# Scaled rows of batches 1 to 3 made on GpSimd, behind the subtraction of their step, instead of on ScalarE

## The chip, the cores and the metric

One core of a Trainium2 chip runs the kernel. The metric is the device time of one execution in microseconds (us), the median of several runs. The engines are TensorE (PE; its weight loads are PEld), VectorE (DVE), ScalarE (ACT), GpSimd (POOL) and SyncE (SP). Each works through its own list of instructions in order; they meet at semaphores.

## What is computed

Four batches of 256 tokens, 256 wide, go through two residual layers:

```
# layer 1: a sparse learned adjacency mixed with the normalised rows
sim  = (ctx Wq^T)(ctx Wk^T)^T * scale            # 256 x 256 per batch
A    = sigmoid(sim) where sim >= 76th largest of its row, else 0
x1   = x + (1-gamma) * layernorm(x) + gamma * (A + A^T) / 2
# layer 2: eight experts of 256 -> 256 -> 256, the best two of each token
xn   = layernorm(x1)
comb = weights of the two best gates of xn @ gate_w, zero for the rest, times alpha
out  = x1 + sum_e comb[e] * (gelu(xn @ fc1[e] + b1[e]) @ fc2[e] + b2[e])
```

`x + (1-gamma) * layernorm(x)` is, for each row, a factor times x plus a constant. These are the "scaled rows" of the title: `x_sb[b,t] = x_sb[b,t] * mul1 + add1`, with one `mul1` and one `add1` for each token.

## The kernel before

Tokens lie on the 128 partitions, so that a batch is 2 tiles of 128x256. All eight experts are computed for every token. Products of expert layers run on TensorE in a split form: each factor has a rounded part (`_hi`) and a remainder (`_lo`), and three products (hi·hi, lo·hi, hi·lo) are summed, which makes 12 matmuls of 256 columns for an `up` (L438, to `p_h`) and 12 for a `down` (L462, to `p_y`).

The expert part is one loop over 32 steps s = 8 b + e (batch b, expert e), written out by hand on each engine. TensorE does `up(s)` and, two steps later (LAG = 2), `down(s)`: the slot of step s holds `up(s)`, then `down(s - 2)`. ScalarE does `gelu(s)` (L576, to `h_act`) and `hidden_hi(s)` (L586, to `h_hi`). GpSimd does `hidden_lo(s)` (L708, the subtraction `h_lo = h_act - h_hi`). VectorE adds the weighted result of `down(s - 2)` to `acc` (`add_expert`, L1071).

The preparation of the next batch is woven into these steps. For batch b + 1, in the steps of batch b:

- e = 0 to 3, VectorE: search of the 76th largest value (counts, MAX8, MATCH_REPLACE8), at e = 2 also `ln1_affine` (L801: `mul1` and `add1`, semaphore `ln1_mul`), at e = 3 `choose` (L914) and `mask` (L958: `half = (sim >= threshold) * half`).
- e = 2, ScalarE: `sigmoid(b+1)` (L549, into `half`), then `base(b+1)` (L592), the scaled rows: two ACTIVATE of 128x256, in place in `x_sb`, released by `ln1_mul`.
- e = 3, GpSimd: `add_masked(b+1)` (L702: `x_sb += half`), when `masked` and `base_ready` are there.
- e = 5: TensorE turns `half` (L377) into `p_a`, VectorE adds it (`residual`, L973, to `x1`) and takes the moments; GpSimd computes `rstd` (L664); at e = 6 VectorE normalises (`normalise`, L987, to `xn`); at e = 7 TensorE transposes `xn` behind `up` (L386) and ScalarE and VectorE split it for the next batch (`xt_hi`, `xt_lo`).

Batch 0 is prepared ahead of the loop. Its scaled rows are made on GpSimd already, by a function of the same name (L682), with TENSOR_SCALAR; its `ln1_affine` is on GpSimd too (L690).

In the first batch the weights are still being split. For experts 2 to 7 ScalarE writes `-w_hi` into `w_lo` (`weight_neg`, L562), and GpSimd issues a DMA that adds `w` to it in memory (`weight_rest`, L673); for experts 4 to 7 it stands behind `hidden_lo` in steps 0 to 3. `up(e)` waits for its landing (L445). In step 4 ScalarE rounds the second biases (`b2_hi`, L649), and in step 5 VectorE combines them with two inputs in SBUF (`b2_parts_of`, L1059) ahead of `residual(1)`. Three more waits matter: `down(s)` waits until `add_expert(s - 2)` is done (L469), `gelu(s)` waits for `hidden_lo(s - 2)` (L580), and `up(s)` for `gelu(s - 2)` (L447).

Of the kernel before, what the change touches and what calls it, by code (L numbers as in the profile page):

```python
# [15 lines left out]
ACT = mybir.ActivationFunctionType  # L16
# [43 lines left out]
def xattn_moe_program(nc, x, attn, small, w, b2, out):  # L60
# [8 lines left out]
    TILES = N // P  # L69
# [13 lines left out]
    with ExitStack() as ctx:  # L83
        def sb(name, shape, dt=F32):
            return ctx.enter_context(nc.sbuf_tensor(name, shape, dt))
# [4 lines left out]
        def sem(name):  # L90
            return ctx.enter_context(nc.semaphore(name))
# [4 lines left out]
        x_sb = sb("x_sb", [P, BATCHES, TILES, HID])  # L96
# [52 lines left out]
        mul1 = sb("mul1", [P, BATCHES, TILES])  # L149
        add1 = sb("add1", [P, BATCHES, TILES])  # L150
# [93 lines left out]
        ln1_mul = sem("ln1_mul")  # L244
        base_ready = sem("base_ready")
# [268 lines left out]
        def _(act):  # L514
# [54 lines left out]
            def xt_hi_of(b):  # L569
                if b >= 2:  # L570
                    act.wait_ge(h_ready, (b - 1) * EXPERTS)
                for k in range(CH):
                    act.wait_ge(xn_t, b * CH + k + 1)
                    nc.scalar.activation(xt_hi[:, b % 2, k], XT_BANKS[k][:, 0:N], ACT.Copy).then_inc(xt_hi_ready, 1)
# [14 lines left out]
                    act.wait_ge(y_ready, s - LAG)  # L589
                nc.scalar.activation(h_hi[:, s % (LAG + 1)], h_act[:, s % 2], ACT.Copy).then_inc(h_hi_ready, 1)  # L590

            def base(b):  # L592

                act.wait_ge(ln1_mul, b + 1)
                for t in range(TILES):
                    last = nc.scalar.activation(x_sb[:, b, t], x_sb[:, b, t], ACT.Identity,
                                                scale=mul1[:, b, t:t + 1], bias=add1[:, b, t:t + 1])
                last.then_inc(base_ready, 1)

            def comb_hi_of(b):  # L600
                act.wait_ge(comb_tr, b + 1)
                nc.scalar.activation(comb_hi[:], COMB_T, ACT.Copy).then_inc(comb_hi_ready, 1)
# [26 lines left out]
            for s in range(STEPS):  # L629
                b, e = divmod(s, EXPERTS)  # L630
                more = b + 1 < BATCHES
                if e == 7 and more:
                    xt_hi_of(b + 1)
                gelu(s)
                if e == 0:
                    act.wait_ge(logits_t_ready, b + 1)
                    nc.scalar.activation(logits_t[:], LOGITS_T, ACT.Copy).then_inc(logits_t_copied, 1)
                hidden_hi(s)
                if e == (2 if b else 1):

                    act.wait_ge(gap_ready, b + 1)
                    nc.scalar.activation(gap_th[:], gap[:], ACT.Tanh, scale=0.5).then_inc(gap_th_ready, 1)
                if s < 2:
                    weight_neg(4 + s)
                if s in (1, 3):
                    weight_neg(6 + s // 2)
                if s == 4:
                    act.wait_ge(b2_in, 16)
                    nc.scalar.activation(b2_hi[:], b2_sb[:], ACT.Copy).then_inc(b2_hi_ready, 1)  # L649
                if e == 2 and more:  # L650
                    sigmoid(b + 1)
                    base(b + 1)
                if e == 5:
                    comb_hi_of(b)
                if e == 4 and b + 2 < BATCHES:
                    spread_of(b + 2)
                if e == 6 and b + 2 < BATCHES:
                    signs_of(b + 2)
                if e == 7 and b + 2 < BATCHES:
                    signs_again_of(b + 2)  # L660

        @block.gpsimd
        def _(pool):
            def rstd(veps, rs, b, veps_ready, ready):  # L664

                pool.wait_ge(veps_ready, (b + 1) * TILES)
                nc.gpsimd.tensor_tensor(rs[:, b, :], veps[:, b, :], neg_half[:], ALU.pow).then_inc(ready, 1)  # L667

            def weight_hi(e):
                pool.wait_ge(w_in[e], 16)  # L670
                nc.gpsimd.tensor_copy(w_hi[:, e], w_sb[:, e]).then_inc(w_hi_early, 1)  # L671

            def weight_rest(e):  # L673
                pool.wait_ge(w_neg_ready, e - 1)
                nc.gpsimd.dma_start(w_lo[:, e], w[:, e].bitcast(F32R), accum_op=ALU.add).then_inc(w_rest_in[e], 16)  # L675

            def weight_lo(e, j):
                pool.wait_ge(w_hi_early, e + 1)
                nc.gpsimd.tensor_tensor(w_lo[:, e, j], w_sb[:, e, j], w_hi[:, e, j],  # L679
                                        ALU.subtract).then_inc(w_lo_ready[e][j], 1)  # L680

            def base(b):  # L682

                pool.wait_ge(ln1_mul, b + 1)
                for t in range(TILES):
                    last = nc.gpsimd.tensor_scalar(x_sb[:, b, t], x_sb[:, b, t], mul1[:, b, t:t + 1],
                                                   add1[:, b, t:t + 1], ALU.mult, ALU.add)
                last.then_inc(base_ready, 1)

            def ln1_affine(b):  # L690

                pool.wait_ge(gam_ready, 1)
                pool.wait_ge(ln1_agg, (b + 1) * TILES)
                pool.wait_ge(ln1_rstd, b + 1)
                for t in range(TILES):
                    nc.gpsimd.tensor_scalar(mul1[:, b, t:t + 1], rstd1[:, b, t:t + 1], gam[:, 2:3], ones[:], ALU.mult,
                                            ALU.add)
                    last = nc.gpsimd.tensor_scalar(add1[:, b, t:t + 1], mv1[:, b, t, 0:1], gam[:, 3:4],
                                                   rstd1[:, b, t:t + 1], ALU.mult, ALU.mult)
                last.then_inc(ln1_mul, 1)  # L700

            def add_masked(b):  # L702

                pool.wait_ge(masked, (b + 1) * TILES)
                pool.wait_ge(base_ready, b + 1)
                nc.gpsimd.tensor_tensor(x_sb[:, b], x_sb[:, b], half[:, b], ALU.add).then_inc(base_sum, 1)

            def hidden_lo(s):  # L708
                pool.wait_ge(h_hi_ready, s + 1)
                if s > LAG:  # L710
                    pool.wait_ge(y_ready, s - LAG)
                nc.gpsimd.tensor_tensor(h_lo[:, s % (LAG + 1)], h_act[:, s % 2], h_hi[:, s % (LAG + 1)],  # L712
                                        ALU.subtract).then_inc(h_lo_ready, 1)

            nc.gpsimd.memset(neg_half[:], -0.5).then_inc(const_set, 1)
            nc.gpsimd.memset(ones[:], 1.0).then_inc(const_set, 1)
            pool.wait_ge(const_set, 2)
            nc.gpsimd.memset(comb_parts[:].bitcast(F32), 0.0).then_inc(rows_cleared, 1)
            nc.gpsimd.memset(b2_parts[:].bitcast(F32), 0.0).then_inc(rows_cleared, 1)
            weight_hi(0)  # L720
            rstd(veps1, rstd1, 0, ln1_veps, ln1_rstd)
            weight_lo(0, 0)
            weight_hi(1)
            weight_hi(2)
            ln1_affine(0)
            base(0)
            pool.wait_ge(chosen_ready, TILES)
            weight_lo(1, 0)
            weight_rest(2)
            pool.wait_ge(gate_hi_ready, 1)  # L730
            nc.gpsimd.tensor_tensor(gate_parts[:, :, 1], gate_sb, gate_parts[:, :, 0], ALU.subtract).then_inc(
                gate_lo_ready, 1)
            weight_lo(0, 1)
            rstd(veps2, rstd2, 0, ln2_veps, ln2_rstd)
            pool.wait_ge(xn_ready, TILES)
            weight_rest(3)
            weight_lo(1, 1)
            weight_hi(6)
            rstd(veps1, rstd1, 1, ln1_veps, ln1_rstd)
            for s in range(STEPS):  # L740
                b, e = divmod(s, EXPERTS)
                more = b + 1 < BATCHES
                if s < STEPS - 1:
                    hidden_lo(s)
                if s < 4:
                    weight_rest(4 + s)
                if s == 1:
                    weight_hi(7)
                if more and b and e == 0:
                    rstd(veps1, rstd1, b + 1, ln1_veps, ln1_rstd)  # L750
                if more and e == 3:
                    add_masked(b + 1)
                if more and e == 5:
                    rstd(veps2, rstd2, b + 1, ln2_veps, ln2_rstd)
                    pool.wait_ge(xn_ready, (b + 2) * TILES)
# [483 lines left out]
```

## Time and profile before

| | |
|---|---|
| median of 3 runs | 129.93 us (129.92 to 130.35) |
| the profiled execution | 129.84 us |
| its span, first to last instruction | 128.0 us |
| TensorE busy | 119.6 us |
| VectorE busy | 95.3 us |
| ScalarE busy | 85.8 us |
| GpSimd busy | 68.4 us |
| granted TensorE clock, mean | 0.996 of full speed |

The busy times are sums over the span and tell which engine has room, not which one sets the end. For that there is the chain of work that ended last, followed back from the last instruction. 1.84 us of the profiled execution lie outside of the span. Records of neighbouring instructions on one engine overlap by some tenths of a us, since each is a pipeline; the distance between two starts is what an instruction costs its engine.

### The profile page before, as it was taken

How to read it: one execution, taken by the hardware profiler on the slowest of the kernel's cores; microseconds unless marked ns; L12 is line 12 of the kernel's file. 1: busy time of each engine (PE TensorE's matmuls, PEld its weight loads, DVE VectorE, ACT ScalarE, POOL GpSimd, SP SyncE). 2: the span in 40 equal slices, each digit the busy share in tenths (PEclk: the TensorE clock that was granted, in tenths of full speed). 3: DMA queues.
4: the chain of work that ended last, by engine and by line, in shares of the span. 5: the costliest groups of instructions: out<-in, count | busy, mean ns of one | idle time of the engine just before them, and what ended most of it. 6: DMA issues, size and time to landing. Idle time of an engine off the chain costs nothing.

```text
span 128.0 us, 2762 instructions
## 1 busy us (share of the span) xinstructions
PE 119.6 (93%) x901; PEld 109.6 (86%) x901; DVE 95.3 (74%) x399; ACT 85.8 (67%) x210; POOL 68.4 (53%) x72
## 2 busy tenths in 40 slices
PE   6796897899899999999999999999999999999990
PEld 3353565799889999999999999999999999999990
DVE  0068899989976999999979899998766228623481
ACT  4279898899999778464987774857546544555510
POOL 2019987799949644652396256506952544444400
PEclk9999999999999999999999999999999999999998
DMA  1999987675998400010000000200000002000002
GB/s 61 200 365 419 405 321 109 83 145 70 196 177 132 88 0 3 0 60 28 5 0 0 5 0 3 82 3 5 0 0 0 5 0 82 0 5 0 3 0 82
DMA packets 3381, 10.05 MB, mean 78 GB/s; under 512 B 397, under 2 KB 869, under 8 KB 3365
## 3 DMA queue, kind: packets, MB, share of 16 engines
q0 software_dynamic: 864, 3.15, 15.1%
q1 hardware_dynamic: 2500, 6.71, 14.6%
q8 instruction: 7, 0.11, 0.4%
q14 instruction: 10, 0.07, 0.2%
HBM read 8.81 MB, written 1.05 MB: 77 GB/s over the span
## 4 chain that ended last, share of the span: by engine, by line
PE 69%; DVE 8%; DMA 7%; ACT 6%; POOL 4%; issue 2%; DVEq 0%; POOLq 0%
PE p_y L480 31%; PE p_h L458 30%; DMA w_lo<-w 5%; DMA attn_sb<-attn 2%; POOL w_lo L679 2%; DVE acc L1084 2%; ACT act_waste L546 2%; ACT h_act L582 1%; DVE top L907 1%; PE p_g L406 1%; PE p_a L382 1%; POOL h_lo L712 1%; PE p_s L342 1%; ACT h_hi L590 1%; PE p_a L335 1%
## 5 line engine op out<-in xcount | busy, mean ns | idle before, releaser
L712 POOL TENSOR_TENSOR h_lo<-h_act,h_hi 128x512 fp32r<-128x512 f32 x31 | 40.3, 1303 | 41.0 <-ACT h_hi L590 37.2
L582 ACT ACTIVATE h_act<-p_h,small_sb 128x256 f32<-128x256 f32 x64 | 26.7, 468 | 21.9 <-PE p_h L458 21.8
L458 PE MATMUL p_h<-xt_hi,w_hi 128*128 128x256 f32 x128 | 33.3, 282 | 0.8 <-DMA w_lo<-w 0.7
L1084 DVE SCALAR_TENSOR_TENSOR acc<-p_y,comb,acc 128x256 f32<-128x256 f32 x55 | 24.0, 476 | 12.6 <-PE p_y L480 11.9
L458 PE MATMUL p_h<-xt_hi,w_lo 128*128 128x256 f32 x128 | 32.9, 279 | 0.0
L480 PE MATMUL p_y<-w_hi,h_hi 128*128 128x256 f32 x126 | 26.0, 288 | 0.0
L458 PE MATMUL p_h<-xt_lo,w_hi 128*128 128x256 f32 x128 | 25.5, 280 | 0.0
L458 PEld LDWEIGHTS p_h<-xt_hi,w_hi 128*128 128x128 f32 x128 | 24.1, 188 | 1.5 <-DMA w_lo<-w 1.1
L480 PE MATMUL p_y<-w_hi,h_lo 128*128 128x256 f32 x126 | 25.3, 282 | 0.0
L480 PE MATMUL p_y<-w_lo,h_hi 128*128 128x256 f32 x126 | 25.2, 281 | 0.0
L458 PEld LDWEIGHTS p_h<-xt_hi,w_lo 128*128 128x128 f32 x128 | 24.0, 188 | 0.0
L590 ACT ACTIVATE h_hi<-h_act 128x512 fp32r<-128x512 f32 x32 | 20.2, 630 | 0.9
L458 PEld LDWEIGHTS p_h<-xt_lo,w_hi 128*128 128x128 f32 x128 | 19.6, 187 | 0.1
L480 PEld LDWEIGHTS p_y<-w_hi,h_hi 128*128 128x128 f32 x126 | 19.3, 188 | 0.2
L480 PEld LDWEIGHTS p_y<-w_lo,h_hi 128*128 128x128 f32 x126 | 19.4, 188 | 0.0
L480 PEld LDWEIGHTS p_y<-w_hi,h_lo 128*128 128x128 f32 x126 | 19.3, 188 | 0.0
L671 POOL CAST w_hi<-w_sb 128x1024 fp32r<-128x1024 f32 x5 | 5.7, 1151 | 7.6 <-DMA w_sb<-w 7.6
L667 POOL TENSOR_TENSOR rstd<-veps,neg_half 128x2 f32<-128x2 f32 x8 | 6.4, 799 | 1.1 <-DVE veps L782 1.1
L358 PE MATMUL p_y<-warm 128*128 128x256 bf16 x27 | 5.5, 378 | 1.2 <-DVE warm L1096 1.2
L567 ACT ACTIVATE w_lo<-w_hi 128x1024 fp32r<-128x1024 f32 x6 | 6.2, 1047 | 0.5 <-POOL w_hi L671 0.5
L907 DVE MAX8 top<-left 128x8 f32<-128x256 f32 x16 | 5.9, 408 | 0.4 <-DVE left L912 0.4
L675 POOL DMA_DIRECT2D w_lo<-w x6 | 5.5, 913 | 1.1 <-DVE xn L992 1.1
(143 smaller groups left out, 185.2 us busy)
## 6 DMA issues: line engine op xcount, KB each, us to landing
w_sb<-w SPq DMA_DIRECT2D x8, 512.0 KB, 8.5
w_lo<-w POOLq DMA_DIRECT2D x6, 512.0 KB, 5.6
x_sb<-x SPq DMA_DIRECT2D x1, 768.0 KB, 8.7
out<-acc SPq DMA_DIRECT2D x3, 256.0 KB, 2.5
x_sb<-x SPq DMA_DIRECT2D x1, 256.0 KB, 4.3
out<-acc SPq DMA_DIRECT2D x2, 128.0 KB, 2.0
attn_sb<-attn SPq DMA_DIRECT2D x1, 192.0 KB, 4.8
small_sb<-small SPq DMA_DIRECT2D x1, 97.5 KB, 4.4
```

The lines of the kernel that those rows point to most:

```text
L358: nc.tensor.matmul(p_y[1][:, 0:N], warm[:, 0:P], warm[:], start=True, stop=True)
L458: last = nc.tensor.matmul(dst, w_[:, e, 0, k, c * P:(c + 1) * P], v[:, b % 2, k, :], start=n == 0, stop=n == len(trio) - 1)
L480: last = nc.tensor.matmul(dst, v[:, s % (LAG + 1), k, t * P:(t + 1) * P], w_[:, e, 1, k, :], start=n == 0, stop=n == len(trio) - 1)
L567: nc.scalar.activation(w_lo[:, e], w_hi[:, e], ACT.Copy, scale=-1.0).then_inc(w_neg_ready, 1)
L582: last = nc.scalar.activation(h_act[:, s % 2, c], tiled(p_h[s % 2])[:, c, :], ACT.Gelu, bias=b1_sb[:, e, c:c + 1])
L590: nc.scalar.activation(h_hi[:, s % (LAG + 1)], h_act[:, s % 2], ACT.Copy).then_inc(h_hi_ready, 1)
L667: nc.gpsimd.tensor_tensor(rs[:, b, :], veps[:, b, :], neg_half[:], ALU.pow).then_inc(ready, 1)
L671: nc.gpsimd.tensor_copy(w_hi[:, e], w_sb[:, e]).then_inc(w_hi_early, 1)
L675: nc.gpsimd.dma_start(w_lo[:, e], w[:, e].bitcast(F32R), accum_op=ALU.add).then_inc(w_rest_in[e], 16)
L712: nc.gpsimd.tensor_tensor(h_lo[:, s % (LAG + 1)], h_act[:, s % 2], h_hi[:, s % (LAG + 1)], ALU.subtract).then_inc(h_lo_ready, 1)
L907: step_of_tile(nc.vector.max(top[:, t, 8 * r:8 * r + 8], left[:, t]))
L1084: last = nc.vector.scalar_tensor_tensor(acc[:, b % 2, t], tiled(y_bank(s, t))[:, t, :], comb[:, b, t, 0, e:e + 1], so_far, ALU.mult, ALU.add)
```

## The change

On ScalarE the function `base` and its call at e = 2 go. On GpSimd `base(b + 1)`, the function that has served batch 0, is called at e = 2 for batches 1 to 3, behind `hidden_lo(s)` and, in the first batch, behind the DMA issue of `weight_rest(6)`. It waits for `ln1_mul` from VectorE and increments `base_ready`, for which `add_masked` waits on GpSimd itself.

```diff
@@ scalar engine
-            def base(b):
-
-                act.wait_ge(ln1_mul, b + 1)
-                for t in range(TILES):
-                    last = nc.scalar.activation(x_sb[:, b, t], x_sb[:, b, t], ACT.Identity,
-                                                scale=mul1[:, b, t:t + 1], bias=add1[:, b, t:t + 1])
-                last.then_inc(base_ready, 1)
-
@@ scalar engine, loop over s
                 if e == 2 and more:
                     sigmoid(b + 1)
-                    base(b + 1)
@@ gpsimd, loop over s
                 if s == 1:
                     weight_hi(7)
+                if more and e == 2:
+                    base(b + 1)
                 if more and b and e == 0:
                     rstd(veps1, rstd1, b + 1, ln1_veps, ln1_rstd)
```

## Rows read from the trace of the kernel before

**Rows 1.** Chain that ended last, in order of time: start us, us, what.

```profile
31.09 6.54 DMA w_lo<-w
...
37.68 1.69 PE p_h L458 x12
...
120.66 1.44 PE p_y L480 x12
```

**Rows 2.** Groups by line and shape, ScalarE and GpSimd: count | busy us, mean ns.

```profile
L596 ACT ACTIVATE x_sb<-x_sb,add,mul 128x256 f32<-128x256 f32 x6 | 3.3, 592 | 3.2 <-DVE add L807 3.2
...
L686 POOL TENSOR_SCALAR x_sb<-x_sb,mul,add 128x256 f32<-128x256 f32 x2 | 1.1, 552 | 0.1
```

**Rows 3.** Timeline of ScalarE, steps 2 to 5: start us, us, line, what.

```profile
34.41 1.08 ACT L596 ACTIVATE x_sb<-x_sb,add,mul 128x256 f32<-128x256 f32 x2
35.40 0.81 ACT L582 ACTIVATE h_act<-p_h,small_sb 128x256 f32<-128x256 f32 x2
...
40.41 0.81 ACT L582 ACTIVATE h_act<-p_h,small_sb 128x256 f32<-128x256 f32 x2
```

**Rows 4.** Timeline of GpSimd, steps 2 to 5; idle before an instruction in brackets.

```profile
34.45 0.86 POOL L675 DMA_DIRECT2D w_lo<-w  x1
36.97 1.27 POOL L712 TENSOR_TENSOR h_lo<-h_act,h_hi 128x512 fp32r<-128x512 f32 x1 [1.66 <-ACT h_hi L590]
38.20 0.87 POOL L675 DMA_DIRECT2D w_lo<-w  x1
38.81 1.57 POOL L706 TENSOR_TENSOR x_sb<-x_sb,half 128x512 f32<-128x512 f32 x1
40.06 1.57 POOL L712 TENSOR_TENSOR h_lo<-h_act,h_hi 128x512 fp32r<-128x512 f32 x1
41.95 1.29 POOL L712 TENSOR_TENSOR h_lo<-h_act,h_hi 128x512 fp32r<-128x512 f32 x1 [0.33 <-ACT h_hi L590]
```

**Rows 5.** Landing of the DMA issued at 38.20, and TensorE's step 7.

```profile
w_lo<-w POOLq DMA_DIRECT2D x1, 512.0 KB, 5.5
...
44.13 0.28 PE L458 MATMUL p_h<-xt_hi,w_hi 128*128 128x256 f32 x1
```

**Rows 6.** Timeline of VectorE, steps 2 to 6.

```profile
32.98 0.25 DVE L807 TENSOR_SCALAR add<-mv,gam,rstd 128x1 f32<-128x1 f32 x1
...
34.93 0.88 DVE L962 SCALAR_TENSOR_TENSOR half<-sim,threshold,half 128x256 f32<-128x256 f32 x2
...
39.55 2.37 DVE L1063 SCALAR_TENSOR_TENSOR b_parts<-b_hi,small_sb,b_sb 24x256 fp32r<-24x256 f32 x1 [1.25 <-ACT b_hi L649]
...
44.77 0.73 DVE L992 TENSOR_SCALAR xn<-x,mv,rstd 128x256 f32<-128x256 f32 x2
```

**Rows 7.** Timeline of TensorE: the third of four transposes of `xn`, second tile.

```profile
45.77 0.27 PE L394 MATMUL p_x<-small_sb,xn 128*128 128x128 f32 x1
```

**Rows 8.** Timelines of GpSimd and VectorE ahead of the loop; last row: durations min/median/max.

```profile
11.99 2.01 POOL L671 CAST w_hi<-w_sb 128x1024 fp32r<-128x1024 f32 x2
13.29 0.73 DVE L877 SCALAR_TENSOR_TENSOR missed<-count,few 128x2 f32<-128x2 f32 x1
17.09 1.27 POOL L679 TENSOR_TENSOR w_lo<-w_sb,w_hi 128x512 fp32r<-128x512 f32 x1 [0.61 <-DVE chosen L918]
L970 DVE TENSOR_TENSOR x_sb<-x_sb,half x2: 429/663/897, 17.7 to 18.6; 128x256 f32<-128x256 f32 x2
```

**Rows 9.** Timelines of ScalarE, GpSimd, VectorE and TensorE, preparation of batch 2.

```profile
60.18 1.10 ACT L596 ACTIVATE x_sb<-x_sb,add,mul 128x256 f32<-128x256 f32 x2 [1.60 <-DVE add L807]
62.74 1.30 POOL L712 TENSOR_TENSOR h_lo<-h_act,h_hi 128x512 fp32r<-128x512 f32 x1 [4.40 <-ACT h_hi L590]
61.84 0.88 DVE L962 SCALAR_TENSOR_TENSOR half<-sim,threshold,half 128x256 f32<-128x256 f32 x2
62.64 1.85 DVE L1084 SCALAR_TENSOR_TENSOR acc<-p_y,comb,acc 128x256 f32<-128x256 f32 x4
64.89 0.48 PE L480 MATMUL p_y<-w_hi,h_hi 128*128 128x256 f32 x2
```

## The prediction, written before the change was run

> **What bounds the kernel now.** I read the chain that ended last first. From 37.68 to 122.1 us it is TensorE's `up` and `down` products and its small transposes, one behind the other with no other engine between; its entrance is the DMA of one weight remainder, issued by GpSimd at 31.09 and landed at 37.6, for which `up(5)` waited [rows 1]. So two things can make this kernel faster: something that lets that DMA land earlier, or fewer matmuls. And one thing makes it slower: any operand that comes to TensorE late after 37.68. Then I read the other engines' timelines only for that question: at each meeting point with TensorE, how early was the operand.
>
> **What is removed.** Six ACTIVATEs of 592 ns go from ScalarE [rows 2]. In the first batch the pair starts at 34.41 and the `gelu` behind it at 35.40, so ScalarE's list moves up by 0.99 us, until `gelu(5)`, which started at 40.41 and will start at 39.42 [rows 3]; I take it that `up(5)`, begun at 37.68 and 1.69 long [rows 1], has just ended then. In batch 2 (and batch 3 alike) ScalarE also idled 1.60 us for `ln1_mul` ahead of the pair, with `gelu(11)` queued behind [rows 9]; both go. But TensorE waited for neither: it is on the chain without a gap there. Gain at the end: 0. The whole removal lies after the issue at 31.09, so the entrance DMA isn't moved either.
>
> **What is added.** Two TENSOR_SCALARs per batch on GpSimd, the very form that made batch 0's rows, at 552 ns [rows 2], 1.10 us a batch.
>
> *First batch.* `ln1_mul` is there at 33.23 [rows 6]: no wait. The DMA issue at 34.45 occupies the list for 0.61 us (38.20 to 38.81, the same issue), so the pair starts at 35.06 and is done at 36.16. GpSimd idled 1.66 us there, until 36.97 [rows 4]. `hidden_lo(3)` queued behind can start when `h_hi(3)` is there, 36.97 - 0.99 = 35.98, so it starts at about 36.16, 0.8 earlier than before. Behind it stands the DMA issue of the last weight: 36.16 + 1.23 = 37.39 instead of 38.20. Before, it landed after 5.5 us at 43.7 and `up(7)` needed it at 44.13 [rows 5]: 0.4 us of room, now 1.2. Then `add_masked(1)` at 38.0 and `hidden_lo(4)` at 39.25 by the same distances [rows 4].
>
> *Batches 2 and 3.* Here `base` does wait: `ln1_mul` comes where ScalarE started its pair, at 60.18, so GpSimd works on the pair until 61.28, with `hidden_lo(11)` queued behind. `h_hi(11)` is early now, so `hidden_lo(11)` runs 61.28 to 62.6, before it began at 62.74 [rows 9]. The wait replaces a longer one. Cost 0.
>
> **A cost that no single row of the moved operation shows.** VectorE instructions that read two SBUF tensors get stuck behind GpSimd work. A 429 ns addition took 897 ns when a GpSimd subtraction ran from 17.09 to 18.36, ending 0.3 us after it; a 128x2 operation took 0.73 us from 13.29 and ended at 14.02, where GpSimd's CASTs (one input) ended at 14.00 [rows 8]; and `b2_parts_of`, on only 24 partitions, took 2.37 us from 39.55 to 41.92, through two GpSimd instructions back to back, and ended in the 0.33 us gap ahead of the third [rows 4, 6]. So a new GpSimd instruction is priced between 0 and its whole length for VectorE (the CAST is the nearest row to TENSOR_SCALAR: full length), and in the other direction GpSimd may be held for as long as a VectorE pair of that kind takes. Three places:
>
> - `mask(1)`, 34.93 to 35.81 [rows 6], meets the new pair from 35.06. Either it goes first and GpSimd's list slips by D, up to about 0.7 us, or its second tile waits until `hidden_lo(3)` ends, about 37.4. `add_masked` then slips with it, but stays near its old 38.81.
> - `mask(2)` at 61.84 meets `hidden_lo(11)`, which was later before. Held until 62.6 plus 0.3, the masks end at 63.3 to 63.8 instead of 62.72. The two accumulations behind them (half of the 1.85 us [rows 9]) end by 64.3 to 64.7, and `down(11)` needs them at 64.89. Room 0.2 to 0.6 us: cost 0, but thin. Batch 3 repeats it.
> - `b2_parts_of` can now begin at 39.55 - 0.99 = 38.56. `add_masked(1)` is running since 38.0, so it is held until a gap. `hidden_lo(4)` lasts to 40.5 to 40.8 (39.25 plus 1.29 or 1.57) and `hidden_lo(5)` starts at 41.95 - 0.99 = 40.96. The gap is 0.15 to 0.4 us; it ends near 41.2, 0.7 earlier than before.
>
> The last one matters since from it hang `residual(1)`, the moments, `rstd` and `normalise(1)`; `xn` was finished at 45.50, and TensorE took its second tile at 45.77 [rows 6, 7]. That is 0.27 us of room, the tightest place of the trace.
>
> The Trainium skill ("SBUF — State Buffer", section "Who interferes with whom") says that the port pair shared by VectorE and GpSimd goes for one whole instruction to whichever issues first. Read so, `b2_parts_of` would get through between `add_masked` and `hidden_lo(4)`, and no gap would be needed. The trace disagrees: it stayed held across two instructions (39.55 to 41.92). By the page the result is no change too; by the row, a rival is alive.
>
> **Sum.** TensorE's chain before 37.68: 0. TensorE's chain after it: 0 from ScalarE, 0 from the pair, 0 from the three meetings. 129.84 us in the profiled execution, of which 128.0 are span; it lies 0.09 under the median, so I forecast the median: 129.9 us.
>
> **Rivals.**
>
> 1. *The gap closes (slower).* If D is between about 0.2 and 0.5, `hidden_lo(4)` ends behind 40.96 and `hidden_lo(5)` follows without a gap. The same happens if `mask(1)`'s second tile is the one held, since `b2_parts_of` then only begins at about 39.6. It is held until `hidden_lo(5)` ends at 42.3 to 42.6, and ends at 42.6 to 42.9 instead of 41.92. `xn` comes 0.7 to 1.0 later, less the room of 0.27: TensorE stands for 0.4 to 0.7 us at 45.55. Time 130.3 to 130.7. For it: the estimates of the gap are as small as 0.15 us, and the row of 2.37 us shows the holding. Against it: with D under 0.2 the gap stays, and with D over about 0.55 `add_masked` starts behind 38.56, so that `b2_parts_of` slips in while GpSimd issues its DMA. 22%.
> 2. *The pair is much slower in the loop than in batch 0 (slower).* It decides from 36.97 + 0.43 - 35.06 = 2.3 us for the pair, over twice its measured 1.10, since then the last weight lands after 44.13. With each tile held as the 897 ns addition was, it is 1.8: not reached. At three times the price, 3.3 us, `up(7)` stands 1.0 us: 130.9. 3%.
> 3. *Freed ScalarE lets TensorE run closer (faster).* It would need a TensorE wait on ScalarE after 37.68; the chain has none. If the last weights' transfers moved the entrance by as much as the issue moved, 0.8 us, it would be 129.1, but that issue stands behind the entrance. 4%.
> 4. *The masks of batches 2 and 3 come late (slower):* past 64.89 by up to 0.3 us, twice: 130.5 at most. 3%.
>
> That the change doesn't do what it says has no place of its own: the only case would be `base` waiting on GpSimd for longer than ScalarE did, and it waits for the same signal.
>
> **How the numbers follow.** No change 68%, its own range 129.7 to 130.3 (the spread of the runs); rivals 22, 3, 4 and 3%. The range takes in rival 1 and the spread below: 129.6 to 130.7. A measurement of this kernel tells about 0.5%, 0.65 us, so the border lies at 130.58: a quarter to a third of rival 1, all of rival 2 and a rest for what isn't foreseen make slower 14%; rival 3 and as small a rest 5% faster; within 0.5% 81%.
>
> **What would show it.** Right: ScalarE's ACTIVATE group of the scaled rows gone and eight TENSOR_SCALARs of about 0.55 us on GpSimd; the DMA issue at about 37.4 to 38.1; `b2_parts_of` over before 41.9; TensorE without a gap from 37.7 on; the span 128.0. Rival 1: a TensorE gap ahead of the transposes of `xn` near 45.6, and `b2_parts_of` ending with `hidden_lo(5)`. Rival 2: a gap ahead of `up(7)` put down to the DMA. Rival 4: a gap ahead of `down` near 65 and 90. I am wrong altogether if `up(5)` no longer starts near 37.7.

## The result and the profile after

The changed kernel takes 130.74 us (median of 5 runs, 130.70 to 131.00) against 129.93 us before: ratio 1.0068, 95% interval 1.0056 to 1.0080. It is 0.8 us slower, where the forecast was no change and the range ended at 130.7. The profiled execution took 131.0 us with a span of 129.2.

The page after: busy time, and the groups that answer to [rows 2]. ScalarE's group of the scaled rows is gone, and GpSimd's has eight instructions instead of two.

```profile
PE 120.3 (93%) x901; PEld 109.9 (85%) x901; DVE 99.5 (77%) x399; ACT 83.2 (64%) x204; POOL 71.8 (56%) x78
...
L677 POOL TENSOR_SCALAR x_sb<-x_sb,mul,add 128x256 f32<-128x256 f32 x8 | 4.9, 639 | 3.8 <-PE p_y L480 1.9
```

ScalarE has lost 2.6 us of busy time and GpSimd gained 3.4. The line to stop at is VectorE's: 4.2 us more, in a change that gives it nothing to do.

The chain that ended last (start us, us, what), which answers to [rows 1]:

```profile
34.87 1.68 PE p_h L458 x12
36.55 1.44 PE p_y L480 x12
37.99 0.03 issue
38.02 0.04 DVE acc L1077
38.05 0.36 issue
38.42 0.48 DVE acc L1077
38.89 1.48 DVE b_parts L1056
40.37 2.65 issue
43.01 0.73 DVE x L971 x2
...
45.55 0.48 DVE acc L1077
46.03 0.33 DVE xn L985
46.36 0.14 issue
46.50 0.30 PE p_x L394
```

Before, this chain was TensorE alone from 37.68 on. Now it leaves TensorE at 38.0 and comes back at 46.5: through the bias combination (L1056, which was L1063), residual, moments and `xn`. The 2.65 us of "issue" are time in which the profile names nobody that VectorE waited for, in the middle of one instruction of 24 partitions.

Timelines of VectorE, GpSimd, ScalarE, VectorE again and TensorE at that place, which answer to [rows 3, 4, 6, 7]:

```profile
34.92 0.44 DVE L911 SCALAR_TENSOR_TENSOR chosen<-small_sb,count,top 128x16 f32<-128x16 f32 x1
35.30 1.19 DVE L955 SCALAR_TENSOR_TENSOR half<-sim,threshold,half 128x256 f32<-128x256 f32 x2
...
35.24 1.64 POOL L677 TENSOR_SCALAR x_sb<-x_sb,mul,add 128x256 f32<-128x256 f32 x2
36.80 1.34 POOL L703 TENSOR_TENSOR h_lo<-h_act,h_hi 128x512 fp32r<-128x512 f32 x1
38.04 0.95 POOL L666 DMA_DIRECT2D w_lo<-w  x1
38.67 1.64 POOL L697 TENSOR_TENSOR x_sb<-x_sb,half 128x512 f32<-128x512 f32 x1
39.92 2.88 POOL L703 TENSOR_TENSOR h_lo<-h_act,h_hi 128x512 fp32r<-128x512 f32 x2
...
40.43 0.63 ACT L590 ACTIVATE h_hi<-h_act 128x512 fp32r<-128x512 f32 x1
...
38.81 4.28 DVE L1056 SCALAR_TENSOR_TENSOR b_parts<-b_hi,small_sb,b_sb 24x256 fp32r<-24x256 f32 x1
45.95 0.73 DVE L985 TENSOR_SCALAR xn<-x,mv,rstd 128x256 f32<-128x256 f32 x2
...
46.50 0.30 PE L394 MATMUL p_x<-small_sb,xn 128*128 128x128 f32 x1 [0.77 <-DVE xn L985]
```

The two `hidden_lo` of 39.92 now stand back to back (one row, x2); before there were 0.33 us of idle between them, and the combination had ended there. It begins 0.14 us behind `add_masked` and ends at 43.09, 0.29 us after GpSimd's third instruction ended at 42.80. `xn` is finished at 46.68 instead of 45.50. The last matmul of `up(7)` starts at 45.45, so the transposes could have started near 45.57; they start at 46.50. TensorE stands for 0.93 us. From the first transpose to the end of the last accumulation there are then 80.12 us, against 79.89 before: `down(5)` starts 0.95 us behind the first transpose instead of 0.72, since the bias sums between them (47.10) wait for `comb_parts`, which VectorE finishes behind `xn` at 47.05. That is the other 0.2 us by which this execution is longer.

### The profile page after: what moved, and what is told of

It reads as the page before. It is cut to its first block, busy times and chain, and to the rows that moved or that the text cites. A ratio compares the mean times of both kernels' runs of the same rounds, so it can differ in the third digit from the quotient of the medians.

```text
span 129.2 us, 2762 instructions
## 1 busy us (share of the span) xinstructions
PE 120.3 (93%) x901; PEld 109.9 (85%) x901; DVE 99.5 (77%) x399; ACT 83.2 (64%) x204; POOL 71.8 (56%) x78
## 4 chain that ended last, share of the span: by engine, by line
PE 67%; DVE 12%; issue 5%; DMA 5%; ACT 4%; POOL 4%; DVEq 0%; POOLq 0%
PE p_y L480 29%; PE p_h L458 28%; DMA w_lo<-w 5%; DVE acc L1077 2%; POOL w_lo L670 2%; PE p_y L358 2%; ACT act_waste L546 2%; DVE b_parts L1056 1%; PE p_x L394 1%; DVE top L900 1%; PE p_g L406 1%; POOL h_lo L703 1%; PE p_s L342 1%; PE p_s L434 1%; PE p_a L335 1%
## 5 line engine op out<-in xcount | busy, mean ns | idle before, releaser
L358 PE MATMUL p_y<-warm 128*128 128x256 bf16 x27 | 6.0, 401 | 1.2 <-DVE warm L1089 1.2
L677 POOL TENSOR_SCALAR x_sb<-x_sb,mul,add 128x256 f32<-128x256 f32 x8 | 4.9, 639 | 3.8 <-PE p_y L480 1.9
L670 POOL TENSOR_TENSOR w_lo<-w_sb,w_hi 128x512 fp32r<-128x512 f32 x4 | 5.7, 1429 | 1.0 <-DVE chosen L911 1.0
## 6 DMA issues: line engine op xcount, KB each, us to landing
out<-acc SPq DMA_DIRECT2D x2, 128.0 KB, 2.0
```

What stands on the lines that cost most here:

```text
L358: nc.tensor.matmul(p_y[1][:, 0:N], warm[:, 0:P], warm[:], start=True, stop=True)
```

## The experiments

Each ratio is to the kernel before, run on the same chip. Theory A: the bias combination, held behind GpSimd, delays `xn`.

**e1: the combination behind the residual.**

```diff
@@ VectorE's loop
-                if s == 5:
-                    b2_parts_of()
                 if more and e == 5:
                     residual(nxt)
+                if s == 5:
+                    b2_parts_of()
```

> The changed kernel with one pair of calls on VectorE swapped: in step 5 the combination of the second biases (two SBUF inputs) stands behind residual(1) instead of ahead of it. Theory A (the bias combination, held from 38.8 to 43.1 us behind three GpSimd instructions back to back, delays the residual, the normalisation and so TensorE's transposes of xn): the 0.9 us gap of TensorE near 46 us goes, time 129.8 to 130.0. Rival B (GpSimd's own list is longer and delays rstd or hidden_lo): the gap stays, 130.7. Rival C (the entrance of the chain, up(4) or up(5), moved): 130.7 with the transposes on time.

Measured 129.48 us, ratio 0.9974 (0.9964 to 0.9985). The gap is gone, and the kernel is faster than before, by more than theory A said.

**e2 and e3: one batch alone.** e2 moves the rows of batch 1 alone, e3 those of batches 2 and 3 alone.

```diff
@@ e2, ScalarE's and GpSimd's loops (e3: if b == 0 on ScalarE, b and e == 2 on GpSimd)
                 if e == 2 and more:
                     sigmoid(b + 1)
-                    base(b + 1)
+                    if b:
+                        base(b + 1)
...
+                if s == 2:
+                    base(1)
```

> Only the scaled rows of batch 1 on GpSimd, those of batches 2 and 3 still on ScalarE. Theory A: the whole loss lies in batch 1, 130.7. A rival by which batches 2 and 3 carry a part (their masks held behind hidden_lo until TensorE waits for the accumulation): between 129.9 and 130.6.

> Only the scaled rows of batches 2 and 3 on GpSimd, those of batch 1 on ScalarE as before. Theory A: 129.9, although choose or mask of batch 2 is held by some 0.8 us behind hidden_lo(11); TensorE without a gap after 38 us. The rival by which these batches carry a part: 130.1 to 130.7.

e2: 130.90 us, ratio 1.0078 (1.0062 to 1.0095). e3: 129.97 us, ratio 1.0005 (0.9995 to 1.0015). The whole loss lies in batch 1. In e3 the holding happens too, as e3's timelines of VectorE, GpSimd and TensorE show, and costs nothing:

```profile
61.54 1.13 DVE L921 SCALAR_TENSOR_TENSOR chosen<-small_sb,count,top 128x16 f32<-128x16 f32 x1
63.59 1.85 DVE L1087 SCALAR_TENSOR_TENSOR acc<-p_y,comb,acc 128x256 f32<-128x256 f32 x4
...
61.35 1.29 POOL L713 TENSOR_TENSOR h_lo<-h_act,h_hi 128x512 fp32r<-128x512 f32 x1
...
64.91 0.48 PE L480 MATMUL p_y<-w_hi,h_hi 128*128 128x256 f32 x2
```

A `choose` of 16 columns takes 1.13 us (its second tile 0.22), until `hidden_lo(11)` ends. Half of the four accumulations is over near 64.5, and `down(11)` starts at 64.91.

**e4: the same swap in the kernel before.** Its diff is e1's.

> The kernel before with the same swap as in e1: the bias combination behind residual(1). Theory A: the operand of the transposes comes up to 1 us earlier, but TensorE did not wait for it before, so 129.9. If instead the bias combination cost time in the kernel before already: 129.5 or less.

129.82 us, ratio 0.9998 (0.9988 to 1.0007). The swap alone is worth nothing; e1 gains from the swap and the move together. In e4 the residual is over earlier, but `xn` is finished at 45.40, only 0.1 us earlier than before: `rstd(1)` stands in GpSimd's list behind `hidden_lo(5)` and starts at 43.22, when that ends.

**e5 and e6: the gap filled, nothing moved.** The kernel before, with an idle GpSimd instruction in the gap: in e5 a copy, in e6 a memset of the same width.

```diff
@@ GpSimd's loop (e6: nc.gpsimd.memset(idle_out[:], 0.0))
                 if s < STEPS - 1:
                     hidden_lo(s)
+                if s == 4:
+                    nc.gpsimd.tensor_copy(idle_out[:], idle_in[:])
```

> The kernel before, scaled rows on ScalarE, with one idle GpSimd instruction added: in step 4, behind hidden_lo(4), a copy of 128x768 from SBUF to SBUF that nobody reads (about 0.78 us by the CAST rows, 1.04 us for 1024 columns). It closes the gap of 0.33 us in which the bias combination ended at 41.92. Theory A (the gap decides): the combination is held until hidden_lo(5) ends, 4 us long or more in place of 2.37, TensorE stands 0.7 to 1.1 us ahead of the transposes near 45.6, time 130.6 to 130.9 without anything moved off ScalarE. Rival (something else of the change, such as ScalarE's earlier steps, made the loss): 129.9.

> As e5, but with a GpSimd memset of 128x768 in that place, which writes SBUF and reads nothing. If VectorE's second input is held only by GpSimd reading SBUF, the combination gets through during the memset and the time is 129.9. If any GpSimd work holds it: as e5, 130.6 to 130.9. The Trainium skill (SBUF — State Buffer, Who interferes with whom) says that an instruction with two SBUF inputs contends with a GpSimd instruction that reads SBUF and not with one that only writes: by it 129.9.

e5: 133.17 us, ratio 1.0221 (1.0164 to 1.0279). e6: 129.91 us, ratio 0.9998 (0.9989 to 1.0008). Timelines of GpSimd, VectorE and TensorE, first of e5, then of e6:

```profile
41.26 1.10 POOL L751 COPY idle_out<-idle_in 128x768 f32<-128x768 f32 x1
42.05 1.54 POOL L715 TENSOR_TENSOR h_lo<-h_act,h_hi 128x512 fp32r<-128x512 f32 x1
...
39.50 4.38 DVE L1070 SCALAR_TENSOR_TENSOR b_parts<-b_hi,small_sb,b_sb 24x256 fp32r<-24x256 f32 x1 [1.27 <-ACT b_hi L652]
...
47.29 0.41 PE L397 MATMUL p_x<-small_sb,xn 128*128 128x128 f32 x1 [1.86 <-DVE xn L999]
```

```profile
41.32 1.03 POOL L747 MEMSET idle_out<- 128x768 f32 x1
42.02 1.58 POOL L713 TENSOR_TENSOR h_lo<-h_act,h_hi 128x512 fp32r<-128x512 f32 x1
...
39.60 2.36 DVE L1066 SCALAR_TENSOR_TENSOR b_parts<-b_hi,small_sb,b_sb 24x256 fp32r<-24x256 f32 x1 [1.18 <-ACT b_hi L650]
```

GpSimd is as busy in both. Behind the copy the combination is held through four instructions, until 43.88, with everything else as in the kernel before: the closed gap is enough. Under the memset it comes through at 41.96, as if the gap were open. So it is GpSimd's reading of SBUF that holds it. That is what the Trainium skill ("SBUF — State Buffer", section "Who interferes with whom") says of an instruction with two SBUF inputs, and the trace agrees (2.36 us with the memset, 4.38 with the copy). Its other sentence, that the pair goes to whoever issues first for the whole instruction, is not enough: here the loser was passed over between instructions three times. Why it loses there too, no run shows; back to back means here that GpSimd's next record starts before the last one ends (42.05 against 42.36).

e5 cost 3.2 us, not the 0.7 to 1.1 expected. Part of it is the longer stand, 1.86 us; the rest is in the granted clock. Stretches of e5: us, busy times of PE, PEld, DVE, ACT and POOL, granted clock, DMA share, GB/s.

```profile
44.00:46.00 2.00, 1.42 (x12) 1.22 (x11) 2.00 (x13) 0.05 (x1) 0.32 (x1) 1.00 0.00 0
46.00:48.00 2.00, 0.71 (x5) 0.74 (x5) 2.00 (x7) 1.05 (x4) 0.86 (x2) 0.84 0.00 0
48.00:50.00 2.00, 2.00 (x11) 2.00 (x10) 1.93 (x9) 1.81 (x5) 0.81 (x1) 0.50 0.00 0
50.00:52.00 2.00, 2.00 (x16) 2.00 (x15) 1.87 (x9) 1.20 (x5) 1.30 (x1) 0.81 0.00 0
52.00:54.00 2.00, 2.00 (x19) 1.91 (x18) 1.93 (x9) 1.42 (x4) 0.00 (x0) 1.00 0.01 4
```

After TensorE stood for 1.86 us it ran from 48 to 50 at half clock, 1.2 GHz: 11 matmuls where 19 fit at 2.4. From the first transpose to the end of the last accumulation e5 takes 81.43 us (47.29 to 128.72), the changed kernel 80.12 (46.50 to 126.62): 1.3 us for the clock. One of e5's four executions took 131.87 us at a mean granted clock of 0.997, the other three 133.12 to 133.37 at 0.983 to 0.987, which is the same 1.3 us. After its own stand of 0.93 us the changed kernel kept the clock at 1.00.

**e7: one input in PSUM.** The changed kernel, the combination in its old place.

```diff
@@ ScalarE, step 4, and VectorE's b2_parts_of
                     nc.scalar.activation(b2_hi[:], b2_sb[:], ACT.Copy).then_inc(b2_hi_ready, 1)
+                    nc.scalar.activation(p_s[0:PARTS * EXPERTS, 0:HID], b2_sb[:], ACT.Copy).then_inc(b2_hi_ready, 1)
...
-            nc.vector.scalar_tensor_tensor(b2_parts[...], b2_hi[:], split_sb[...], b2_sb[:], ...)
+            nc.vector.scalar_tensor_tensor(b2_parts[...], b2_hi[:], split_sb[...], p_s[0:PARTS * EXPERTS, 0:HID], ...)
```

> The changed kernel, with the bias combination at its old place but one of its two tensors in PSUM: ScalarE copies the biases there as well in step 4 (24x256, 0.4 us). Theory A (two SBUF inputs are what is held): the combination takes about 0.46 us in place of 4.28 although GpSimd is as busy, TensorE's gap near 46 goes, time 129.5 to 129.9. Rival (VectorE is held by whatever GpSimd does, or TensorE's gap has another cause): 130.7.

129.50 us, ratio 0.9972 (0.9961 to 0.9984). Timeline of VectorE, then of GpSimd:

```profile
38.93 0.47 DVE L1057 SCALAR_TENSOR_TENSOR b_parts<-b_hi,small_sb,p_s 24x256 fp32r<-24x256 f32 x1 [0.55 <-ACT p_s L642]
...
38.60 1.62 POOL L698 TENSOR_TENSOR x_sb<-x_sb,half 128x512 f32<-128x512 f32 x1
39.84 2.87 POOL L704 TENSOR_TENSOR h_lo<-h_act,h_hi 128x512 fp32r<-128x512 f32 x2
```

The same operation at the same place in the order beside the same three GpSimd instructions: 0.47 us instead of 4.28. The second SBUF input is the cause, not GpSimd's work as such.

**e8 and e12: can TensorE's chain be entered earlier?** e8 is e1 with the DMA of expert 4 issued ahead of `hidden_lo(0)`; e12 is e7 with those of experts 4 and 5 early.

```diff
@@ e8: ScalarE ahead of the loop and in step 0, GpSimd ahead of the loop
-            weight_hi(5)
+            weight_neg(4)
...
-                if s < 2:
-                    weight_neg(4 + s)
+                if s == 0:
+                    weight_hi(5)
+                if s == 1:
+                    weight_neg(5)
...
+            weight_rest(4)
@@ e12: as e8, but weight_neg(5) in step 0 and weight_rest(5) ahead of hidden_lo(1)
```

> e1 plus an earlier DMA at the entrance of TensorE's chain: ScalarE negates the rounded part of expert 4 ahead of the loop and rounds expert 5 in step 0 instead (the two trade places), and GpSimd issues the DMA of expert 4 ahead of hidden_lo(0), at about 27.0 in place of 28.8 us. TensorE waited 0.35 us for it in e1 at 34.4. If the entrance bounds e1, the time falls by up to 0.35 to about 129.1 to 129.3; if xn or the DMA of expert 5 binds next, 129.4 to 129.5.

> e7 (the changed kernel, the bias combination reading PSUM, so that xn is ready near 44.2) with the DMAs of experts 4 and 5 issued earlier: that of expert 4 ahead of hidden_lo(0) as in e8, that of expert 5 ahead of hidden_lo(1), at about 29.4 in place of 31.2 us; ScalarE rounds and negates expert 5 in step 0. If the two DMAs are all that holds the entrance, both waits of TensorE (0.3 to 0.4 us near 34 and 37) go: 128.8 to 129.1. If the 1 us more of ScalarE's work in step 0 delays gelu(1) until TensorE waits for it, 129.3 or more.

e8: 129.26 us, ratio 0.9947 (0.9930 to 0.9964), the fastest of all. e12: 129.87 us, ratio 0.9995 (0.9985 to 1.0004). e12 did take both DMA waits away: `up(5)` started at 36.80. But its second outcome came, in another form: ScalarE's extra work in step 0 delays the gate's weights and with them VectorE by 1.0 us. Its second `choose` then begins at 35.88, about when the pair's second tile starts, and is held for 2.14 us (0.44 in the changed kernel), until `hidden_lo(3)` has ended; masks and accumulations come late, and TensorE waits in `down(3)`. Timelines of VectorE, GpSimd and TensorE in e12:

```profile
35.88 2.14 DVE L916 SCALAR_TENSOR_TENSOR chosen<-small_sb,count,top 128x16 f32<-128x16 f32 x1
...
35.28 1.45 POOL L679 TENSOR_SCALAR x_sb<-x_sb,mul,add 128x256 f32<-128x256 f32 x2
36.36 1.63 POOL L705 TENSOR_TENSOR h_lo<-h_act,h_hi 128x512 fp32r<-128x512 f32 x1
...
39.76 0.48 PE L480 MATMUL p_y<-w_hi,h_hi 128*128 128x256 f32 x2 [0.44 <-DVE acc L1083]
...
41.28 0.28 PE L458 MATMUL p_h<-xt_hi,w_hi 128*128 128x256 f32 x1
```

`up(6)` starts at 41.28, as in the kernel before (41.29): the whole gain is given back within one step. This is the holding of the bias combination over again, at another instruction. Here GpSimd's list does not slip (1.08 us for the pair), and VectorE pays instead.

**e9 to e11, e13 and e14: where e1's extra 0.3 us come from.** e9 is e2 with the swap, e10 is e3 with the swap, e11 is e4 with an idle memset on GpSimd where the pair of batch 1 would stand. e13 and e14 are e9 with one delay put back.

```diff
@@ e11, GpSimd, behind weight_rest(6)
+                if s == 2:
+                    nc.gpsimd.memset(idle_out[:], 0.0)      # 128x1280
@@ e13, GpSimd, behind hidden_lo(3)
+                if s == 3:
+                    nc.gpsimd.memset(idle_out[:], 0.0)      # 128x256
@@ e14, ScalarE, behind weight_neg(7)
+                if s == 3:
+                    nc.scalar.activation(idle_out[:], idle_in[:], ACT.Copy)      # 128x1024
```

> e1 came 0.3 us below e4, though both have the bias combination behind residual(1); up(5) started at 37.35 in e1's profile and at 37.65 in e4's. This kernel: only batch 1's scaled rows on GpSimd, and the swap. Theory D (the 0.3 us belong to the move of batch 1, at the entrance of TensorE's chain): 129.5. Theory E (they belong to batches 2 and 3, where ScalarE no longer waits for mul1 and add1): 129.8.

> Only the scaled rows of batches 2 and 3 on GpSimd, and the swap. Theory D: 129.8, as e4. Theory E: 129.5.

> e4 (all scaled rows of the loop on ScalarE, and the swap) with an idle GpSimd memset of 128x1280, about 1.3 us, where the moved pair of batch 1 stands, behind the DMA issue of expert 6. If a busy GpSimd behind that issue is what lets expert 5's DMA land earlier: 129.5. If it is ScalarE's shorter list in batch 1: 129.8, as e4.

> e9 (batch 1's scaled rows on GpSimd and the swap, 129.54) with one idle GpSimd memset of 128x256, about 0.25 us, ahead of the DMA issue of the last weight in step 3, so that it is issued at 38.2 as in the kernel before, in place of 37.96. Theory F: the 0.3 us by which e9 and e1 lie under e4 come from this DMA, which holds up(7) in e4: 129.7 to 129.85. If it is ScalarE's earlier gelu(4) and gelu(5) instead: 129.5 to 129.6.

> e9 with one idle ScalarE copy of 128x1024, about 1.0 us, behind weight_neg(7) in step 3, so that gelu(4) and gelu(5) run as late as in the kernel before and the last weight's DMA as early as in e9. Theory F: 129.5 to 129.6. If ScalarE's place in steps 4 and 5 is what counts: 129.8.

| | median us | ratio, 95% interval |
|---|---|---|
| e9 | 129.54 | 0.9968, 0.9956 to 0.9979 |
| e10 | 129.81 | 0.9988, 0.9978 to 0.9998 |
| e11 | 129.81 | 0.9990, 0.9980 to 1.0000 |
| e13 | 129.66 | 0.9987, 0.9973 to 1.0001 |
| e14 | 129.72 | 0.9989, 0.9979 to 0.9998 |

The extra belongs to batch 1 (e9, not e10), and a busy GpSimd alone does not bring it (e11). Putting ScalarE's 1.0 us back costs most of the 0.3 us: 0.2 by the medians, and by the ratios all of it (0.9989 against 0.9988 in e10; its interval only touches that of e9). e13 lies between and decides nothing: its runs went from 129.25 to 130.19.

The profiles of e9 and e11 show where the time goes. Both enter `up(5)` at the same time (37.43 and 37.44), but `up(8)` starts at 47.41 in e9 and at 47.64 in e11, and the spans are 127.7 and 128.0. Timelines of GpSimd, VectorE and TensorE, first of e9, then of e11:

```profile
42.37 1.25 POOL L668 TENSOR_TENSOR rstd<-veps,neg_half 128x2 f32<-128x2 f32 x1
...
44.83 0.46 DVE L1059 SCALAR_TENSOR_TENSOR comb_parts<-comb_hi,small_sb,p_g 24x256 fp32r<-24x256 f32 x1
...
43.77 0.19 PEld L458 LDWEIGHTS p_h<-xt_hi,w_hi 128*128 128x128 f32 x1
...
45.66 0.48 PE L434 MATMUL p_s<-b_parts,comb_parts 128*128 128x256 f32 x2
```

```profile
43.26 0.90 POOL L668 TENSOR_TENSOR rstd<-veps,neg_half 128x2 f32<-128x2 f32 x1
...
45.35 0.46 DVE L1059 SCALAR_TENSOR_TENSOR comb_parts<-comb_hi,small_sb,p_g 24x256 fp32r<-24x256 f32 x1
...
43.93 0.19 PEld L459 LDWEIGHTS p_h<-xt_hi,w_hi 128*128 128x128 f32 x1
...
45.86 0.50 PE L435 MATMUL p_s<-b_parts,comb_parts 128*128 128x256 f32 x2
```

About 0.15 us is lost at the first weight load of `up(7)`: in e11 the last weight's DMA was issued at 38.24, in e9 at 37.99, which is theory F. Less than 0.1 us is lost at the bias sums, which start 0.05 us after `comb_parts` is finished in e11 (45.81) and 0.37 us after it in e9 (45.29). `comb_parts` is late in e11 because `rstd(1)` stands behind `hidden_lo(5)`, which waits for ScalarE's `gelu(5)`. So both theories seem to carry a part. This is read from two executions and not tested by itself.

It also explains why other profiles don't show it. The start of `up(5)` varies from one execution to the next, 37.26 to 37.68 with the rows of batch 1 on ScalarE and 37.30 to 37.82 in the changed kernel, e1, e2, e7 and e9. In an execution that enters late (e4 at 37.65, e14 at 37.83) the entrance alone sets the end, 9.95 us from `up(5)` to `up(8)` in both against 10.20 in e11; in one that enters early, a late `xn` or last weight takes the gain back. The shortest runs agree: 129.25 to 129.44 in e1, e7, e9 and e13, but 129.65 to 129.74 in e4, e10, e11 and e14.

## Why the prediction was wrong

- **What bounds the kernel.** Right: TensorE's chain from 37.7, entered through a DMA of the weights, and a loss could only come from an operand that is late after it. It was a single operand, at the place called the tightest, with 0.27 us of room.
- **Removal, gain 0.** ScalarE's list moved up as worked out (`b_hi` at 38.30 instead of 39.12, in an execution whose ScalarE row ran 0.17 later). That TensorE gains nothing from it held only as long as `xn` was bound too. With the combination out of the way the move of batch 1 is worth 0.3 us (e9 against e10), through `rstd(1)` and the last weight's DMA as far as the profiles of e9 and e11 show. Small, but not 0. The rooms of 0.27 and 0.4 us were read in an execution that entered at 37.68; in one that enters earlier they are smaller. In e3, with the combination and batch 1 as before and the entrance at 37.40, `up(7)` to `up(8)` took 3.87 us instead of 3.56.
- **The pair, batches 2 and 3.** Right: 1.10 us at 61.44 in the changed kernel, `choose` held by 0.9 us where the masks were expected to be, no cost (e3).
- **The pair, batch 1.** Its own price was right where nothing met it (1.06 us from start to start at 61.44). D, the slip of GpSimd's list where the pair meets VectorE's two-input instructions, was left open between 0 and 0.7 us. It is 0.46: 35.24 to 36.80 is 1.56 us for 1.10 us of work; the pair met `choose` as well as the masks. GpSimd's row also ran 0.18 later in this execution (35.24 against 35.06). With both, the DMA issue of the last weight came at 38.04, not at 37.39, and `add_masked` at 38.67, not at 38.0. The sum used D = 0 for them without saying why.
- **The step that failed** is the third of the three meetings: "The gap is 0.15 to 0.4 us". That is the gap with D = 0. In the changed kernel `hidden_lo(4)` started at 39.92 instead of 39.25 and lasted until 41.5, and `h_hi(5)` was there at 41.06: no gap. The 0.18 of the later execution moved both alike; D alone closed the gap. Rival 1 names this, with its condition of D between 0.2 and 0.5, and is what happened. It got 22% because two escapes were given the rest. D near 0 was not likely: it needs that the pair doesn't meet the masks, although they start within 0.13 us of each other. The late escape, `add_masked` starting behind the combination, was missed by little: 38.67 against 38.81, and in e2, which is as slow, 38.63 against 38.71. So which side of it the kernel fell on was a matter of a tenth of a us, which the sum could not have told.
- **The size of rival 1** was 0.4 to 0.7 us; TensorE stood for 0.93 in the profiled execution and lost 0.2 more at the bias sums. The combination ended at 43.09 and not at 42.6 to 42.9, since GpSimd's row ran 0.18 later there, while TensorE was only 0.03 later (`up(6)` at 41.32 instead of 41.29). That TensorE also waits for `comb_parts` behind `xn` was in no term. That execution was the longest of the five (131.0 us); the median is 130.74 against 130.7 as the end of the range.
- **The rule of the Trainium skill.** It had been weighed against one row. With it the combination would have passed between two instructions; it was passed over once before, twice in the changed kernel and three times in e5. The row was the better guide.

## What to carry to other kernels

A VectorE instruction with two tensors in SBUF needs a gap in GpSimd's list, not just a free VectorE. Before giving GpSimd work, look for such instructions beside it whose results are due soon, and count GpSimd's idle time there: as long as it is back to back with instructions that read SBUF they don't pass. The remedies measured here, each in the changed kernel, are an input in PSUM (e7, 4.28 to 0.47 us) and another place in VectorE's order (e1). With either, the moved rows make a kernel that is 0.3% faster than the one before (129.50 and 129.48 us; 129.26 in e8, with a weight's DMA earlier as well).

When a sum contains an unknown that decides whether a gap exists, it has to be carried through every later start, and the case where it is 0 is no more likely than the others. A room of some tenths of a us, read in one execution, is worth checking against how much the entrance of the chain varies (here 0.6 us).

## What the runs showed of the hardware

- A VectorE instruction of 24x256 with two inputs in SBUF was held behind three and four GpSimd instructions in a row (4.28 and 4.38 us; 0.47 with one input in PSUM). It ended 0.29 us after the last of them. One of 128x16 was held for 2.14 us (e12).
- A GpSimd memset, 1.03 us long, doesn't hold it; a copy of the same width does (e6, e5).
- Where both start close together both are slowed: of the pair one TENSOR_SCALAR took 938 ns instead of 552, of the masks one took 776 ns instead of 482, and the second `choose` 0.44 us instead of 0.22, in the changed kernel.
- TensorE's granted clock fell to 0.50, 1.2 GHz, behind a stand of 1.86 us, which cost another 1.3 us; behind a stand of 0.93 us it stayed at 1.00.
